# Issuing the moves of h ahead of the column loads, and placing its transposes one half-step later

## The chip, the cores and the metric

The kernel runs on one core of one Trainium2 chip. The metric is the device time of one execution in microseconds (us). Before the change the median of three runs is 1601.92 us (1600.87 to 1601.97).

## The reference, cut to what matters

There are B = 16 sequences x of 512 rows (S) by 512 columns (D), all in f32. Each passes through two parts:

```python
# part A: pooled attention of one sequence, and the layer norm behind it
attn_in = tanh(x @ W1 + b1)                      # 512 x 128
scores  = attn_in @ v                            # 512
p       = softmax(where(mask, scores, -1e30))    # prefix, postfix or cloze mask, by itok
pooled  = (p @ x) / count_of_the_mask            # 512 x 512
h       = layernorm(pooled) * gamma + beta
# part B: feed-forward, F = 2048, weights dequantized from integer codes
y   = silu(h @ w1 + fc1_bias)                    # 512 x 2048
z   = y @ w2 + fc2_bias                          # 512 x 512
out = x + pooled + 0.5 * z
```

## The kernel before, in words

Every matmul of f32 values is made from two parts in the type fp32r: a rounded copy ("hi") and the rest ("lo"). A product takes three matmuls, hi by hi, hi by lo and lo by hi. All dequantized weights stay in SBUF.

The program is written out by hand for each engine; semaphores join the engines. `ffn(b)` exists on TensorE, VectorE and ScalarE and does part B of sequence b, with the steps of part A of sequence a = b + 1 set between. On TensorE it has 28 half-steps h (0 to 27, `LAST`). An even h issues `fc1(b, h/2 + 2)`, 12 matmuls of 512 columns that make one 128-row piece k of the hidden layer in one of two PSUM banks `y_ps` (lines 1045 to 1047). An odd h issues `fc2(b, (h-1)/2)`, 12 matmuls that add piece k into the four banks `z_ps` (lines 1079 to 1081). Behind the half-steps come `fc2(b, 14)`, `fc2(b, 15)`, and `fc1(b+1, 0)` and `fc1(b+1, 1)` of the next sequence. The turn from one sequence to the next is called a transition here.

Between `fc1(b, k)` and `fc2(b, k)` stand two steps. ScalarE's `silu(b, k)` (line 561) waits for the matmuls of fc1 and writes `y_f`; it is placed at the even half-step h = 2(k - 2), so silu(b, 15) stands at h = 26. VectorE's `split_y(b, k)` (lines 849 and 851) makes `y_hi` and `y_lo` from it; it waits for silu and for `fc2(b, k-2)`, whose operands it overwrites. It is placed at h = 2(k - 1): split_y(b, 14) at h = 26, split_y(b, 15) at h = 28. Each engine runs its own list strictly in order. At every half-step the silu or split comes first and then the steps which the tables `ACT_STEADY` and `DVE_STEADY` name for that half-step.

The layer norm of the next sequence ends on VectorE with `normalise` (step "H", h = 20, line 800). The transposed h that fc1 needs is reached in one of two ways. For a = 0 and a = 1 TensorE transposes it (`by_pe`). For a = 2 to 15 it goes by these steps:

- `move_h(a)` on SyncE (line 364) waits for `h_ready` and issues 16 DMAs of 64 KB from `scratch` to `h_cols`; they move blocks of 32 by 32 to their transposed places.
- `turn_h(a, c)`, "TURNH" on VectorE (line 807): four transposes within the blocks, `h_cols` to `scratch`. The first waits until all 16 moves have landed (`h_moved`).
- `h_scaled_rows(a, c)`, "AFFINE" on ScalarE (line 551): four times gamma and beta, in place.
- `split_h(a, c)` on VectorE (lines 814 and 816): `hT_hi` and `hT_lo`. c = 0 and 1 stand in the table ("SPLITH", h = 27, so ahead of split_y(b, 15)), c = 2 and 3 behind the loop.

TURNH and AFFINE both stand at h = 25, so ahead of split_y(b, 14) on VectorE and ahead of silu(b, 15) on ScalarE.

SyncE issues the other DMAs too. `turn(b, p)` is its list for one sequence, run for b = 1 to 14: wait until the pooling matmuls of sequence b have read `xs_hi` and `xs_lo` (`xs_used`; `x_cols` lies in the same memory), issue the 16 pieces of 64 KB of `load_columns(b + 1)` (line 323), then `move_h(b)` where b is 2 or more, then four stores of sequence b - 1 (line 328) and four loads of x of sequence b + 1 (line 376). `move_h(15)` stands alone behind the list. The `x_cols` are read by VectorE's "TURN" (line 686) at h = 0 to 2 of `ffn(b)`, which is the half-step 0 of the sequence after the moves. `h_cols` lies in the memory of `part_hi`, `part_lo`, `coef` and `u_rows`.

Of the kernel before, what the change touches and what calls it, by code (L numbers as in the profile page):

```python
# [18 lines left out]
def build(nc, x, itok, cond_w, cond_b, cond_v, gamma, beta, fc1_q, fc1_s, fc1_b, fc2_q, fc2_s, fc2_b, out):  # L19
# [16 lines left out]
    with ExitStack() as ctx:  # L36
# [112 lines left out]
        def bank(name):  # L149
# [106 lines left out]
                     17: [("PZ", 2)], 18: [("PZ", 3)]}  # L256
        ACT_STEADY = {0: [("XT", 0)], 1: [("XT", 1)], 2: [("XT", 2)], 3: [("XT", 3)], 4: [("TANH", 0)], 5: [("SC", 0)],
                      9: [("EXPE", 0), ("EXP", 0)], 11: [("U", 0)], 15: [("PZ", 0)], 16: [("PZ", 1)], 17: [("PZ", 2)],
                      18: [("PZ", 3)], 25: [("AFFINE", 0), ("AFFINE", 1), ("AFFINE", 2), ("AFFINE", 3)]}
        DVE_STEADY = {0: [("TURN", 0), ("TURN", 1), ("XT", 0)], 1: [("TURN", 2), ("XT", 1)], 2: [("TURN", 3), ("XT", 2)],  # L260
                      3: [("XT", 3)], 4: [("PAR", 0)], 5: [("SCAN", 0)], 6: [("COLS", 0)], 7: [("ROWMAX", 0)],
# [3 lines left out]
                      25: [("TURNH", 0), ("TURNH", 1), ("TURNH", 2), ("TURNH", 3)], 27: [("SPLITH", 0), ("SPLITH", 1)]}  # L265

        def by_pe(a):
            return isinstance(a, int) and a <= 1
# [39 lines left out]
        @block.sync  # L308
        def _(sp):
            x_dram = x.rearrange("b (j p) d -> (b j) p d", p=P)  # L310
            out_dram = out.rearrange("b (j p) d -> (b j) p d", p=P)

            def load_x(a, p, blocks):
                for J in blocks:
                    sp.dma_start(xt[p][:, J, :], x_dram[bass.ds(a * NJ + J, 1), :, :].rearrange("a p d -> p (a d)")).then_inc(x_in[p][J], 16)

            x_split = x.rearrange("b (i q) d -> b q i d", q=Q)

            def load_columns(a):
                for s in range(ND):  # L320
                    for j in range(P // Q):
                        cols = slice(s * P + j * Q, s * P + (j + 1) * Q)
                        sp.dma_start(x_cols[s][j * Q:(j + 1) * Q, :].rearrange("q (i d) -> q i d", d=Q),  # L323
                                     x_split[bass.ds(a, 1), :, :, cols].rearrange("a q i d -> q (a i) d")).then_inc(cols_in[s], 16)

            def store(b, p, J):
                sp.wait_ge(final_done, b * NJ + (J + 1))
                sp.dma_start(out_dram[bass.ds(b * NJ + J, 1), :, :].rearrange("a p d -> p (a d)"), xt[p][:, J, :]).then_inc(stored[J], 16)

            NG = NF // ND  # L330

            def load_w1(g):
                cols = slice(g * NG * P, (g + 1) * NG * P)
                sp.dma_start(q1[:, :, cols], fc1_q[:, cols].rearrange("(c p) f -> p c f", p=P)).then_inc(w1_in[g], 16)
                sp.dma_start(s1[:, :, cols], fc1_s[:, cols].rearrange("(o k) f -> o k f", o=1).to_broadcast([P, ND, NG * P])).then_inc(w1_in[g], 16)

            def load_w2(g):
                rows = slice(g * NG, (g + 1) * NG)
                sp.dma_start(q2[:, rows, :], fc2_q[g * NG * P:(g + 1) * NG * P, :].rearrange("(k p) d -> p k d", p=P)).then_inc(w2_in[g], 16)
                sp.dma_start(s2[:, rows, :], fc2_s[rows, :].rearrange("(o k) d -> o k d", o=1).to_broadcast([P, NG, D])).then_inc(w2_in[g], 16)  # L340

            load_x(0, 0, range(2))
            sp.dma_start(wc_f.rearrange("p (c a) -> p c a", c=ND), cond_w.rearrange("(c p) a -> p c a", p=P)).then_inc(wc_in, 16)
            sp.dma_start(tok_i[:], itok.rearrange("(o d) -> o d", o=1).to_broadcast([P, B])).then_inc(tok_in, 16)
            load_x(0, 0, range(2, NJ))
            load_w1(0)
            load_w2(0)
            sp.dma_start(b2h[:], fc2_b.rearrange("(o d) -> o d", o=1).to_broadcast([P, D])).then_inc(bias_in, 16)
            load_w1(1)
            load_x(1, 1, range(NJ))  # L350
            load_w2(1)
            sp.wait_ge(xs_used, NJ)
            load_columns(1)
            for g in range(2, ND):
                load_w1(g)
                load_w2(g)

            def move_h(a):
                rows = scratch[:, 0:NJ * D].rearrange("p (n d) -> p n d", d=P)
                sp.wait_ge(h_ready, a * NJ + NJ)  # L360
                for i in range(P // Q):
                    for j in range(P // Q):
                        piece = slice(j * Q, (j + 1) * Q)
                        sp.dma_start(h_cols[piece, :, i * Q:(i + 1) * Q], rows[i * Q:(i + 1) * Q, :, piece]).then_inc(h_moved, 16)  # L364

            def turn(b, p):

                sp.wait_ge(xs_used, (b + 1) * NJ)
                load_columns(b + 1)
                if not by_pe(b):  # L370
                    move_h(b)
                for J in range(NJ):
                    store(b - 1, p, J)
                for J in range(NJ):
                    sp.wait_ge(stored[J], b * 16)
                    sp.dma_start(xt[p][:, J, :], x_dram[bass.ds((b + 1) * NJ + J, 1), :, :].rearrange("a p d -> p (a d)")).then_inc(x_in[p][J], 16)

            turn(1, 0)
            turn(2, 1)
            with sp.Fori(1, B // 2 - 1) as i:  # L380
                turn(i * 2 + 1, 0)
                turn(i * 2 + 2, 1)
            move_h(B - 1)
            for b in (B - 2, B - 1):
                for J in range(NJ):
                    store(b, b % 2, J)
            for J in range(NJ):
                sp.wait_ge(stored[J], 16 * B)
# [786 lines left out]
```

## Time and profile before

| what | value |
|---|---|
| median of three runs | 1601.92 us |
| the profiled execution's own time | 1604.28 us |
| its span, first to last instruction | 1602.5 us |
| TensorE busy in the span | 1578.7 us (99%) |
| VectorE busy | 954.0 us (60%) |
| ScalarE busy | 431.6 us (27%) |
| mean granted TensorE clock | 0.999 |

"Busy" counts a matmul from its start to its modelled end, 0.39 us; when matmuls follow one another without a gap, the next one starts after 0.2267 us, while the one before still counts as busy. An idle time of TensorE in a row therefore leaves out the first 0.16 us of each gap.

### The profile page before, as it was taken

Reading aid. Unit: us, or ns where it says so; the run is one execution under the profiler, and the core shown is the slowest. Engines: PE = TensorE matmul, PEld = TensorE weight load, DVE = VectorE, ACT = ScalarE, POOL = GpSimd, SP = SyncE. Lnnn points to the kernel's source line nnn. Section 1 sums busy time; section 2 is a strip of 40 time slices with the busy share of each in tenths; the row PEclk is TensorE's granted clock in tenths of the full one; section 3 lists DMA queues with packets and bytes.
Section 4 is the critical chain, followed back from the end, with each engine's and each line's share of the span. In section 5 each row is a group of like instructions: output and inputs, shape, how many; then the busy total and the mean of one; then the engine's idle time right before and its main releaser. Section 6 shows DMA issues by size and latency. Waiting matters only on the chain.

```text
span 1602.5 us, 20995 instructions
## 1 busy us (share of the span) xinstructions
PE 1578.7 (99%) x7259; PEld 1268.9 (79%) x7259; DVE 954.0 (60%) x1918; ACT 431.6 (27%) x662; POOL 177.8 (11%) x156
## 2 busy tenths in 40 slices
PE   8999999999999999999999999999999999999999
PEld 5778788787887778787787877877878777887887
DVE  7896556655665565646656466555655656456522
ACT  3552322222231222312322223222222323123211
POOL 4101011110101101011110111101111010110100
PEclk9999999999999999999999999999999999999999
DMA  8803031130312204031040311303112031220200
GB/s 282 231 1 79 1 53 53 25 81 1 53 54 37 69 1 87 20 50 57 4 104 1 53 53 18 90 1 53 53 32 75 1 66 41 45 62 0 53 1 27
DMA packets 271311, 82.75 MB, mean 52 GB/s; under 512 B 247498, under 2 KB 248036, under 8 KB 270692
## 3 DMA queue, kind: packets, MB, share of 16 engines
q1 hardware_dynamic: 271152, 81.31, 21.4%
q8 instruction: 67, 1.10, 0.3%
q14 instruction: 40, 0.33, 0.1%
q10 hardware_dynamic: 52, 0.01, 0.0%
HBM read 49.83 MB, written 16.78 MB: 42 GB/s over the span
## 4 chain that ended last, share of the span: by engine, by line
PE 71%; SPq 14%; DVE 9%; issue 4%; DMA 2%; ACT 1%; DVEq 0%; ACTq 0%
PE y_ps L1045 11%; PE y_ps L1046 11%; PE y_ps L1047 11%; PE z_ps L1079 10%; PE z_ps L1080 9%; PE z_ps L1081 9%; SPq L364 8%; SPq L323 6%; DMA h_cols<-scratch 2%; DVE scratch L807 2%; DVE y_lo L851 1%; PE a_ps L1009 1%; PE a_ps L1011 1%; PE a_ps L1010 1%; PE a_ps L961 1%
## 5 line engine op out<-in xcount | busy, mean ns | idle before, releaser
L1079 PE MATMUL z_ps<-w_hi,y_hi 128*128 128x512 f32 x1024 | 402.0, 393 | 7.3 <-DVE y_lo L851 6.7
L1045 PE MATMUL y_ps<-hT_hi,w_hi 128*128 128x512 f32 x1016 | 406.4, 400 | 1.1 <-DVE w_lo L835 0.5
L561 ACT ACTIVATE y_f<-y_ps,vec_cols 128x512 f32<-128x512 f32 x256 | 176.2, 688 | 853.0 <-PE y_ps L1047 842.0
L1080 PE MATMUL z_ps<-w_lo,y_hi 128*128 128x512 f32 x1024 | 399.0, 390 | 0.0
L1081 PE MATMUL z_ps<-w_hi,y_lo 128*128 128x512 f32 x1024 | 398.9, 390 | 0.0
L1047 PE MATMUL y_ps<-hT_hi,w_lo 128*128 128x512 f32 x1016 | 396.9, 391 | 0.0
L1046 PE MATMUL y_ps<-hT_lo,w_hi 128*128 128x512 f32 x1016 | 396.9, 391 | 0.0
L1045 PEld LDWEIGHTS y_ps<-hT_hi,w_hi 128*128 128x128 f32 x1016 | 191.2, 188 | 60.2 <-issue 21.0
L1079 PEld LDWEIGHTS z_ps<-w_hi,y_hi 128*128 128x128 f32 x1024 | 192.3, 188 | 56.7 <-DVE y_lo L851 16.6
L1046 PEld LDWEIGHTS y_ps<-hT_lo,w_hi 128*128 128x128 f32 x1016 | 191.3, 188 | 41.8 <-issue 3.4
L1081 PEld LDWEIGHTS z_ps<-w_hi,y_lo 128*128 128x128 f32 x1024 | 192.3, 188 | 40.2
L1080 PEld LDWEIGHTS z_ps<-w_lo,y_hi 128*128 128x128 f32 x1024 | 192.4, 188 | 39.1 <-issue 0.2
L1047 PEld LDWEIGHTS y_ps<-hT_hi,w_lo 128*128 128x128 f32 x1016 | 191.1, 188 | 40.6
L849 DVE CAST y_hi<-y_f 128x512 fp32r<-128x512 f32 x240 | 112.8, 470 | 182.9 <-PE z_ps L1081 143.9
L851 DVE TENSOR_TENSOR y_lo<-y_f,y_hi 128x512 fp32r<-128x512 f32 x256 | 178.5, 697 | 20.7 <-ACT y_hi L480 12.4
L414 POOL TENSOR_TENSOR x<-x,scratch 128x512 f32<-128x512 f32 x64 | 83.2, 1302 | 872.6 <-ACT scratch L539 872.6
L422 POOL TENSOR_TENSOR x<-x,b2h 128x512 f32<-128x512 f32 x64 | 83.2, 1334 | 451.1 <-DVE hT_lo L816 413.3
L780 DVE BATCH_NORM_STATS2 stats<-scratch 128x6 f32<-128x512 f32 x64 | 44.4, 693 | 112.5 <-ACT scratch L539 112.5
L807 DVE STREAM_TRANSPOSE scratch<-h_cols 128x512 f32<-128x512 f32 x56 | 34.9, 680 | 87.3 <-DMA h_cols<-scratch 87.3
L539 ACT ACTIVATE scratch<-a_ps,columns 128x512 f32<-128x512 f32 x64 | 44.1, 689 | 97.1 <-PE a_ps L1014 95.3
L719 DVE TENSOR_TENSOR_SCAN scratch<-scratch 128x512 f32<-128x512 f32 x15 | 18.4, 1226 | 84.3 <-ACT scratch L480 84.3
L551 ACT ACTIVATE scratch<-scratch,vec_cols 128x512 f32<-128x512 f32 x56 | 41.1, 805 | 67.1 <-DVE scratch L807 67.1
(208 smaller groups left out, 1187.7 us busy)
## 6 DMA issues: line engine op xcount, KB each, us to landing
x<-in_x_dram SPq DMA_DIRECT2D x64, 256.0 KB, 3.4
out_dram<-x SPq DMA_DIRECT2D x64, 256.0 KB, 2.2
x_cols<-in_x_dram SPq DMA_DIRECT2D x240, 64.0 KB, 2.2
h_cols<-scratch SPq DMA_DIRECT2D x224, 64.0 KB, 2.1
fc_codes<-in_L_ffn_fc_q_dram SPq DMA_DIRECT2D x8, 1024.0 KB, 14.9
fc_scaled<-in_L_ffn_fc_scales_dram SPq DMA_DIRECT2D x8, 1024.0 KB, 16.3
scratch<-in_L_cond_W_dram SPq DMA_DIRECT2D x1, 256.0 KB, 4.3
b2h<-in_L_ffn_fc_bias_dram SPq DMA_DIRECT2D x1, 256.0 KB, 15.7
```

Source lines behind the costliest of these rows:

```text
L323: sp.dma_start(x_cols[s][j * Q:(j + 1) * Q, :].rearrange("q (i d) -> q i d", d=Q), x_split[bass.ds(a, 1), :, :, cols].rearrange("a q i d - ...
L364: sp.dma_start(h_cols[piece, :, i * Q:(i + 1) * Q], rows[i * Q:(i + 1) * Q, :, piece]).then_inc(h_moved, 16)
L414: nc.gpsimd.tensor_tensor(xt[p][:, J, :], xt[p][:, J, :], pooled[J], ALU.add).then_inc(res_added, 1)
L561: nc.scalar.activation(y_f[k % 2][:], y_ps[k % 2][:], ACT.Silu, bias=b1[:, k:k + 1]).then_inc(silu_done, 1)
L849: v.tensor_copy(y_hi[k % 2][:], y_f[k % 2][:]).then_inc(yhi_done, 1)
L851: v.tensor_tensor(y_lo[k % 2][:], y_f[k % 2][:], f32(y_hi[k % 2][:]), ALU.subtract).then_inc(split_done, 1)
L1045: mm(o, w1_hi[:, c, cols], hT_hi[:, c, :], start=(c == 0), stop=False)
L1046: mm(o, w1_hi[:, c, cols], hT_lo[:, c, :], start=False, stop=False)
L1047: last = mm(o, w1_lo[:, c, cols], hT_hi[:, c, :], start=False, stop=(c == ND - 1))
L1079: mm(z_ps[r][:], y_hi[k % 2][:, rows], w2_hi[:, k, :], start=(k == 0), stop=False)
L1080: mm(z_ps[r][:], y_hi[k % 2][:, rows], w2_lo[:, k, :], start=False, stop=False)
L1081: last = mm(z_ps[r][:], y_lo[k % 2][:, rows], w2_hi[:, k, :], start=False, stop=(k == NF - 1))
```

## The change

Two edits. In the tables of the steady sequences, the four steps AFFINE of ScalarE and the four steps TURNH of VectorE go from half-step 25 to 26. Since the silu and the split of a half-step come first, AFFINE then stands behind silu(b, 15) and TURNH behind split_y(b, 14). In SyncE's `turn`, `move_h(b)` goes ahead of the wait for `xs_used` and of `load_columns(b + 1)`.

```diff
         ACT_STEADY = {...
-                      18: [("PZ", 3)], 25: [("AFFINE", 0), ("AFFINE", 1), ("AFFINE", 2), ("AFFINE", 3)]}
+                      18: [("PZ", 3)], 26: [("AFFINE", 0), ("AFFINE", 1), ("AFFINE", 2), ("AFFINE", 3)]}
         DVE_STEADY = {...
-                      25: [("TURNH", 0), ("TURNH", 1), ("TURNH", 2), ("TURNH", 3)], 27: [("SPLITH", 0), ("SPLITH", 1)]}
+                      26: [("TURNH", 0), ("TURNH", 1), ("TURNH", 2), ("TURNH", 3)], 27: [("SPLITH", 0), ("SPLITH", 1)]}
...
             def turn(b, p):
 
+                if not by_pe(b):
+                    move_h(b)
                 sp.wait_ge(xs_used, (b + 1) * NJ)
                 load_columns(b + 1)
-                if not by_pe(b):
-                    move_h(b)
                 for J in range(NJ):
                     store(b - 1, p, J)
```

## Rows read from the trace of the kernel before

**Rows 1.** The page, busy time, share and count of TensorE.
```profile
PE 1578.7 (99%) x7259; PEld 1268.9 (79%) x7259; DVE 954.0 (60%) x1918; ACT 431.6 (27%) x662; POOL 177.8 (11%) x156
```

**Rows 2.** TensorE's waits from 200 to 1560 us: us in total, times, longest.
```profile
PE z_ps L1079 <- DVE y_lo L851: 6.7, 14, 1.3
```

**Rows 3.** Timeline of TensorE at one transition: start us, us, [idle before <-releaser].
```profile
527.70 0.39 PE L1079 MATMUL z_ps<-w_hi,y_hi 128*128 128x512 f32 x1
...
530.19 0.39 PE L1081 MATMUL z_ps<-w_hi,y_lo 128*128 128x512 f32 x1
531.30 0.50 PE L1079 MATMUL z_ps<-w_hi,y_hi 128*128 128x512 f32 x1 [0.72 <-DVE y_lo L851]
531.64 0.40 PE L1080 MATMUL z_ps<-w_lo,y_hi 128*128 128x512 f32 x1
...
533.92 0.39 PE L1081 MATMUL z_ps<-w_hi,y_lo 128*128 128x512 f32 x1
534.49 0.50 PE L1079 MATMUL z_ps<-w_hi,y_hi 128*128 128x512 f32 x1 [0.18 <-DVE y_lo L851]
```

**Rows 4.** The same timeline one transition earlier, end of fc2(b, 14), start of fc2(b, 15).
```profile
435.82 0.39 PE L1081 MATMUL z_ps<-w_hi,y_lo 128*128 128x512 f32 x1
436.32 0.50 PE L1079 MATMUL z_ps<-w_hi,y_hi 128*128 128x512 f32 x1
```

**Rows 5.** Timeline of VectorE around the transition of rows 3.
```profile
511.66 1.91 DVE L800 TENSOR_SCALAR scratch<-scratch,mv,columns 128x512 f32<-128x512 f32 x4
...
519.80 0.43 DVE L849 CAST y_hi<-y_f 128x512 fp32r<-128x512 f32 x1 [4.29 <-PE z_ps L1081]
...
527.72 2.49 DVE L807 STREAM_TRANSPOSE scratch<-h_cols 128x512 f32<-128x512 f32 x4 [6.76 <-DMA h_cols<-scratch]
...
531.16 0.42 DVE L814 CAST hT_hi<-scratch 128x512 fp32r<-128x512 f32 x1
...
533.29 0.42 DVE L849 CAST y_hi<-y_f 128x512 fp32r<-128x512 f32 x1
533.75 0.69 DVE L851 TENSOR_TENSOR y_lo<-y_f,y_hi 128x512 fp32r<-128x512 f32 x1
...
544.78 0.70 DVE L686 STREAM_TRANSPOSE scratch<-x_cols 128x512 f32<-128x512 f32 x1
```

**Rows 6.** Timeline of ScalarE around the transition of rows 3.
```profile
522.46 0.69 ACT L561 ACTIVATE y_f<-y_ps,vec_cols 128x512 f32<-128x512 f32 x1 [4.75 <-PE y_ps L1047]
528.47 2.93 ACT L551 ACTIVATE scratch<-scratch,vec_cols 128x512 f32<-128x512 f32 x4 [5.32 <-DVE scratch L807]
531.31 0.67 ACT L561 ACTIVATE y_f<-y_ps,vec_cols 128x512 f32<-128x512 f32 x1
```

**Rows 7.** Timeline of SyncE's DMA issues, same transition: start us, us.
```profile
506.07 8.74 SPq L323 DMA_DIRECT2D x_cols<-in_x_dram  x16
514.96 11.27 SPq L364 DMA_DIRECT2D h_cols<-scratch  x16
538.51 2.16 SPq L328 DMA_DIRECT2D out_dram<-x  x4
```

**Rows 8.** The same, the longest issue of 16 moves among the 14.
```profile
905.48 11.80 SPq L364 DMA_DIRECT2D h_cols<-scratch  x16
```

**Rows 9.** Timelines at the last transition: SyncE's moves, VectorE's transposes, TensorE's fc2(b, 15).
```profile
1489.52 11.34 SPq L364 DMA_DIRECT2D h_cols<-scratch  x16
...
1502.34 2.49 DVE L807 STREAM_TRANSPOSE scratch<-h_cols 128x512 f32<-128x512 f32 x4 [5.29 <-DMA h_cols<-scratch]
...
1509.00 0.40 PE L1081 MATMUL z_ps<-w_hi,y_lo 128*128 128x512 f32 x1
1509.23 0.39 PE L1079 MATMUL z_ps<-w_hi,y_hi 128*128 128x512 f32 x1
```

**Rows 10.** The page, DMA issues: count, KB each, median us from issue to landing.
```profile
x_cols<-in_x_dram SPq DMA_DIRECT2D x240, 64.0 KB, 2.2
h_cols<-scratch SPq DMA_DIRECT2D x224, 64.0 KB, 2.1
```

## The prediction, made before the changed kernel was run

> **What bounds the kernel now.** I read the page first: TensorE is busy 1578.7 of 1602.5 us [rows 1]. So at most 24 us of visible idle can be had, and only what sits on TensorE counts. The waits came next, cut to the part behind the start-up (200 us on). The reader is to see that one wait is left there: fc2's first matmul for VectorE's y_lo, 14 times, 6.7 us in all [rows 2]. Third, the timeline of TensorE at a transition, where those waits lie. In a stream without gaps matmuls start 0.2267 us apart: 11 such steps lead from 527.70 to 530.19 [rows 3]. At the transition the first matmul of fc2(b, 14) starts 531.30 - 530.19 = 1.11 us after the one before it, which is 0.88 too much, the next one 0.34 after that, 0.11 too much, and fc2(b, 15) starts 534.49 - 533.92 = 0.57 after, 0.34 too much, with another 0.11 behind it. This transition loses 1.45 us, though its rows show only 0.72 + 0.18 as idle.
>
> Why: both wait for split_y. VectorE stands from 520.96 in front of TURNH, whose data land only at 527.72, and split_y(b, 14) is queued behind the four transposes [rows 5]. Its input (silu of 522.46 [rows 6]) and its buffer have been ready for long: the cast of split_y(b, 13) ran at 519.80 [rows 5], released by fc2, and one pair of half-steps is 24 x 0.2267 = 5.44 us, so split_y(b, 14) could run at 525.24. On ScalarE silu(b, 15) is queued behind the four AFFINE: it could run at 522.46 + 5.44 = 527.90 and runs at 531.31 [rows 6].
>
> **The whole loss.** There are 14 transitions by way of the moves (into sequences 2 to 15). Seven have two visible waits each: these are the 14 waits of 6.7 us in all. Each hides a further 0.39 - 0.23 = 0.16 us and costs 0.11 at the restart: 6.7 + 14 x 0.27 = 10.5 us. In six, only fc2(b, 15) is late and too little to show as idle: 436.32 - 435.82 = 0.50 us, 0.27 too much [rows 4], and 0.11 at the restart: 6 x 0.38 = 2.3 us. The last transition has no loss: 1509.23 - 1509.00 = 0.23 [rows 9]. Sum: 12.8 us.
>
> **What decides about a transition.** Call T the start of TURNH. In the old order fc2(b, 15) starts at T + 6.77 (534.49 - 527.72 [rows 3, 5]). In the last transition T = 1502.34 and the matmul is due at 1509.23, 6.89 later, so nothing waits [rows 9]. There SyncE had no column pieces ahead of its moves, and T is 1502.34 - 1489.52 = 12.82 us behind the first issue. This is the price of the moves in the changed order, already measured once.
>
> **First edit, the order on SyncE.** h is ready at 511.66 + 1.91 = 513.57 [rows 5]; the moves are first issued at 514.96, because the 16 pieces occupy the queue until 514.81 [rows 7]. Now they start at about 513.6, 1.3 us earlier. With 12.82 us from first issue to T, T = 526.4; with the longest issue seen (11.80 for 11.34 [rows 8, 9]) 526.9. The moves alone would by T + 6.77 put fc2(b, 15) at 533.2 to 533.7, against a due time of 527.70 + 5.44 = 533.14: most of the loss gone by this edit alone, a few tenths a transition left.
>
> Where a move's completion stands in relation to the pieces ahead of it, the trace shows 2.1 us from issue to landing as the median over all 224 moves [rows 10], and the last transition's moves, with nothing ahead of them, land no sooner: the last of 16 issues in 11.34 us starts about 0.7 before 1500.86, and T is 1502.34, 2.2 later [rows 9]. The Trainium skill (DMA: Bandwidth & Descriptors, Queues, rings and completion order) says that a semaphore increment lands only after every earlier write of the same DMA engine; by that the moves' count would be held up by column pieces ahead of them, and the edit would gain latency as well as queue time. The trace does not agree that any is to be had: by the rule T comes still earlier and rival 1 would have hardly a chance, by the rows it doesn't, and I take the rows.
>
> What is moved past what: the 16 column pieces, the wait for xs_used (fulfilled long before h is ready, since the pieces start at 506.07) and their landing now come behind the moves. Issue from 513.6 + 11.3 = 524.9 (525.4 with 11.80), 8.74 us long [rows 7], so until 533.6 to 534.2, landed 2.2 later [rows 10], 536. They are read by TURN at 544.78 [rows 5], in the faster kernel at 543.3: 7 us to spare. The stores behind them on SyncE's queue start at 538.51 [rows 7], about 537.1 then: 3 us to spare. Both cost nothing while this cover lasts. Bounds: 0, and 1 us a transition for each us by which the pieces land later than 543.3. I take 0; the pieces have to go wrong by 7 us.
>
> **Second edit, the order on VectorE and ScalarE.** split_y(b, 14) runs at 525.24 and takes 0.46 + 0.69 us [rows 5], done at 526.4. fc2(b, 14) is due at 527.70 + 2.72 = 530.42, so its wait is gone with 4 us to spare, whatever the moves do. TURNH then starts at the later of 526.4 and the landing, also 526.4 to 526.9. What is late next is fc2(b, 15), by one of two chains:
> - By VectorE: TURNH 2.49, two split_h 533.29 - 531.16 = 2.13, split_y(b, 15) 0.46 + 0.69, and 0.05 to the matmul [rows 3, 5], in all 5.82. For 533.14 T has to be at most 527.32. There are 0.4 to 0.9 us to spare.
> - By ScalarE: silu(b, 15) at 527.90, 0.69 long; AFFINE from 528.6, the first ends after 0.8 (2.93 for four [rows 6], one start each 0.7), at 529.4; then 2.13 + 1.15 + 0.05 as before: 532.7. 0.4 us to spare.
>
> So AFFINE behind silu(b, 15) costs nothing: it would start at 528.47 in the old order [rows 6], 528.6 in the new. The last two split_h run from 532.6 to 534.8, and fc1(b+1, 0) is due at 533.14 + 2.72 = 535.86, needing its fourth chunk 2 us after that. Without the first edit T would stay 527.72 and fc2(b, 15) would come at 533.5, 0.4 late: the second edit alone keeps a loss of about 0.4 + 0.11 in the seven bad transitions. Bounds of this edit: nothing lost, or, if ScalarE's chain takes 0.7 us more than summed, 0.3 + 0.11 in each of 14, 5.7 us.
>
> **Sum.** No instruction is added or taken away; 12.8 us of gaps go. The profiled execution, 1604.28 us with a span of 1602.5, would become 1591.5 and 1589.7. The runs have a median of 1601.92, 2.4 lower than the profiled one; the gaps are the same in kind, so the median becomes 1601.92 - 12.8 = 1589.1. In the gapless stream at 0.23 instead of 0.2267 per matmul around transitions there may be another 1 or 2 us either way.
>
> **Rivals.**
> 1. fc2(b, 15) stays late. For it: both chains have only 0.4 us of slack, built of ten small instructions. Against it: all their durations come from the same place of the trace. Price 0.41 x 14 = 5.7 us: 1594.8.
> 2. The loss is only handed on, and TensorE waits just as long somewhere behind the transition, or SyncE spends the 1.3 us in longer issues (the same 16 moves took 11.27, 11.80 and 11.34 us). Against it: the last transition, which has the new order on SyncE, has neither wait. Price: the gain, 12.8 us; 1601.9, or 1599 where a part is kept.
> 3. Slower: the column pieces come too late for TURN, VectorE stands in front of it at half-step 0 and the splits behind it on VectorE starve fc2. It begins to cost when the pieces land after 543.3, and outweighs the gain when they are late by more than 12.8 / 13 = 1.0 us in each of the 13 turns that have both moves and pieces, landing after 544.3 against 536 as summed. With 2 us of lateness: 1589.1 + 26 = 1615. For it: issue times on this queue scatter. Against it: by a few us at most in 16 issues.
>
> **How the numbers follow.** A measurement of this kernel tells about 0.2%, 3.2 us, from no change. The forecast, all gaps gone, 1586.5 to 1591.5: chance 0.63. Rival 1, about 1592 to 1597: 0.20. Rival 2: 0.11, of which 0.02 still faster. Rival 3: 0.06. Faster by over 0.2% is 0.63 + 0.20 + 0.02 = 0.85, within 0.2% 0.09, slower 0.06. Range: 1586.5 to 1595.5, which holds the forecast's case and most of rival 1.
>
> **What would show it.** In the trace after: no wait of fc2 for y_lo behind 200 us (14 before); the cast of split_y(b, 14) 5.44 us behind that of split_y(b, 13) and ahead of TURNH; moves issued within 0.1 us of the end of line 800, pieces behind them; T about 12.8 us behind the first move; matmul starts 0.23 apart through the transition; TURN without a wait for a DMA. The prediction is wrong if fc2(b, 15) still waits, if TURN waits for x_cols, or if the gaps are gone and the span is not 11 to 14 us shorter.

## The result and the profile after

The changed kernel takes 1589.71 us, the median of four runs (1589.08 to 1590.59), against 1601.95 us for four runs of the kernel before: 12.2 us less, ratio 0.9918 (95% interval 0.9905 to 0.9930). The forecast was 1589.1, the range 1586.5 to 1595.5. Run again in a later set it had a median of 1589.92 beside 1603.31, ratio 0.9915 (0.9901 to 0.9928).

The page after, busy times; 6.5 us less of busy TensorE time for the same 7259 matmuls, the part of the gaps which counts as busy [rows 1].
```profile
span 1587.8 us, 20995 instructions
PE 1572.2 (99%) x7259; PEld 1270.0 (80%) x7259; DVE 952.1 (60%) x1918; ACT 431.8 (27%) x662; POOL 178.1 (11%) x156
```

TensorE's waits between 200 and 1545 us: after, the view has no row, and fc2 waits for VectorE nowhere. Before, it has the row of 6.7 us in 14 times [rows 2] and a second one:
```profile
PE y_ps L1045 <- issue: 0.4, 2, 0.2
```
These two waits lie at the jumps of TensorE's loop (639.43 and 834.76), where the changed kernel's profile has gaps too small to show; they differ from profile to profile and have nothing to do with the edits.

The same transition as in rows 3, now about 3.6 us earlier on the clock. TensorE: end of fc2(b, 14), start of fc2(b, 15).
```profile
526.82 0.39 PE L1079 MATMUL z_ps<-w_hi,y_hi 128*128 128x512 f32 x1
...
529.32 0.39 PE L1081 MATMUL z_ps<-w_hi,y_lo 128*128 128x512 f32 x1
529.54 0.39 PE L1079 MATMUL z_ps<-w_hi,y_hi 128*128 128x512 f32 x1
529.77 0.39 PE L1080 MATMUL z_ps<-w_lo,y_hi 128*128 128x512 f32 x1
```
Where rows 3 have 0.57 and 0.34 us between starts, these have 0.22 and 0.23.

VectorE, to be read against rows 5:
```profile
508.06 1.91 DVE L800 TENSOR_SCALAR scratch<-scratch,mv,columns 128x512 f32<-128x512 f32 x4
...
516.21 0.43 DVE L849 CAST y_hi<-y_f 128x512 fp32r<-128x512 f32 x1 [4.29 <-PE z_ps L1081]
...
521.65 0.43 DVE L849 CAST y_hi<-y_f 128x512 fp32r<-128x512 f32 x1 [4.29 <-PE z_ps L1081]
522.11 0.69 DVE L851 TENSOR_TENSOR y_lo<-y_f,y_hi 128x512 fp32r<-128x512 f32 x1
522.72 2.48 DVE L807 STREAM_TRANSPOSE scratch<-h_cols 128x512 f32<-128x512 f32 x4
525.82 0.43 DVE L814 CAST hT_hi<-scratch 128x512 fp32r<-128x512 f32 x1 [0.61 <-ACT scratch L551]
...
527.95 0.42 DVE L849 CAST y_hi<-y_f 128x512 fp32r<-128x512 f32 x1
528.40 0.69 DVE L851 TENSOR_TENSOR y_lo<-y_f,y_hi 128x512 fp32r<-128x512 f32 x1
```
The cast of split_y(b, 14) comes 521.65 - 516.21 = 5.44 us behind the one before and ahead of TURNH. TURNH no longer waits for the moves. The wait has gone to the first split of h, 0.61 us for AFFINE, which costs nothing: split_y(b, 15) ends at 529.09, 0.05 is the way to the matmul, and fc2(b, 15) is due at 529.54. This is a slack of 0.4 us.

ScalarE and SyncE, to be read against rows 6 and 7:
```profile
524.30 0.69 ACT L561 ACTIVATE y_f<-y_ps,vec_cols 128x512 f32<-128x512 f32 x1 [4.75 <-PE y_ps L1047]
524.89 2.92 ACT L551 ACTIVATE scratch<-scratch,vec_cols 128x512 f32<-128x512 f32 x4
```
```profile
510.00 11.06 SPq L364 DMA_DIRECT2D h_cols<-scratch  x16
521.35 8.34 SPq L323 DMA_DIRECT2D x_cols<-in_x_dram  x16
533.42 2.16 SPq L328 DMA_DIRECT2D out_dram<-x  x4
```
The moves start 0.03 us behind the end of line 800 (508.06 + 1.91 = 509.97), and the pieces end 3.7 us before the stores begin.

How much of the time it is: 13 whole sequences, from the scores of sequence 2 to those of sequence 15 (first column), before and after. Columns: stretch, its length, then busy times.
```profile
171.19:1439.99 1268.80, 1261.04 (x5799) 1014.51 (x5798) 753.06 (x1547) 328.17 (x507) 132.63 (x104) 1.00 0.20 44
```
```profile
170.85:1425.33 1254.48, 1254.48 (x5800) 1015.49 (x5799) 751.18 (x1547) 328.31 (x507) 132.74 (x104) 1.00 0.20 44
```
14.3 us went in these 13 sequences. In the other runs of this study the same stretch tells more than the whole time, since the first sequence varies by 1.2 us from one profile to another (91.8 or 93.0 us from its scores to the next). The same kernel profiled twice differs by 0.7 us in it (1254.48, and 1255.15 for `again` below).

Counted from start to start, some 11 us of other gaps behind 200 us are left in the changed kernel. They stand at the same places as before, 0.8 us a sequence, the largest 0.41 us right behind the score matmuls; the change does not touch them.

### The profile page after: what moved, and what is told of

It reads as the page before. It is cut to its first block, busy times and chain, and to the rows that moved or that the text cites. A ratio compares the mean times of both kernels' runs of the same rounds, so it can differ in the third digit from the quotient of the medians.

```text
span 1587.8 us, 20995 instructions
## 1 busy us (share of the span) xinstructions
PE 1572.2 (99%) x7259; PEld 1270.0 (80%) x7259; DVE 952.1 (60%) x1918; ACT 431.8 (27%) x662; POOL 178.1 (11%) x156
## 4 chain that ended last, share of the span: by engine, by line
PE 93%; DVE 5%; ACT 1%; issue 1%; DMA 0%; SPq 0%; DVEq 0%; ACTq 0%
PE y_ps L1045 14%; PE z_ps L1079 14%; PE z_ps L1080 14%; PE z_ps L1081 14%; PE y_ps L1046 14%; PE y_ps L1047 14%; PE a_ps L1009 1%; PE a_ps L1014 1%; PE a_ps L1011 1%; PE a_ps L1010 1%; PE a_ps L960 1%; PE a_ps L962 1%; PE a_ps L961 1%; PE a_ps L977 1%; PE a_ps L966 1%
## 5 line engine op out<-in xcount | busy, mean ns | idle before, releaser
L849 DVE CAST y_hi<-y_f 128x512 fp32r<-128x512 f32 x240 | 109.6, 457 | 246.7 <-PE z_ps L1081 204.0
L860 DVE TENSOR_TENSOR x<-z_ps,x 128x512 f32<-128x512 f32 x64 | 40.0, 683 | 20.5 <-PE z_ps L1081 20.5
L691 DVE TENSOR_TENSOR part_lo<-scratch,part_hi 128x512 fp32r<-128x512 f32 x30 | 20.7, 690 | 48.7 <-ACT part_hi L480 48.7
## 6 DMA issues: line engine op xcount, KB each, us to landing
b2h<-in_L_ffn_fc_bias_dram SPq DMA_DIRECT2D x1, 256.0 KB, 15.6
```

What stands on the lines that cost most here:

```text
L849: v.tensor_copy(y_hi[k % 2][:], y_f[k % 2][:]).then_inc(yhi_done, 1)
```

## The experiments

Theory A: a transition costs what VectorE's split_y(b, 15) comes too late for fc2(b, 15), and that follows from T, the start of TURNH, by a chain whose length the order of steps sets: T + 6.77 in the old order, T + 5.8 in the new; the order on SyncE sets T. The rivals: one of the two edits carries the gain; the slack is nothing; the wait is handed on. Medians of five runs or more; the kernel before ran beside each, in three sets on three chips, and its medians differ by 0.6 us between them. "13 seq." is the stretch of above.

| kernel | median | before | ratio (95%) | 13 seq. |
|---|---|---|---|---|
| sp_only | 1592.10 | 1603.46 | 0.9930 (0.9917 to 0.9944) | 1255.90 |
| steps_only | 1593.71 | 1603.46 | 0.9939 (0.9925 to 0.9953) | 1259.30 |
| sp_turnh | 1589.98 | 1603.46 | 0.9915 (0.9902 to 0.9929) | 1255.34 |
| sp_affine | 1591.18 | 1603.46 | 0.9926 (0.9913 to 0.9940) | 1256.18 |
| again (the changed kernel) | 1589.92 | 1603.31 | 0.9915 (0.9901 to 0.9928) | 1255.15 |
| more_work | 1603.23 | 1603.31 | 0.9999 (0.9990 to 1.0008) | 1268.36 |
| cols_behind_stores | 1598.36 | 1603.31 | 0.9973 (0.9963 to 0.9983) | 1262.99 |
| cols_behind_loads | 1655.98 | 1603.31 | 1.0329 (1.0315 to 1.0343) | 1320.36 |
| split_behind | 1589.77 | 1603.89 | 0.9912 (0.9899 to 0.9926) | 1255.07 |
| split_behind_sp | 1590.26 | 1603.89 | 0.9916 (0.9902 to 0.9929) | 1254.29 |

### Each edit alone

sp_only, the changed kernel with the steps put back:
```diff
-26: [("AFFINE", 0), ...]      -26: [("TURNH", 0), ...]
+25: [("AFFINE", 0), ...]      +25: [("TURNH", 0), ...]
```


> Only the moves of h go ahead of the column pieces; TURNH and AFFINE stay at half-step 25. Theory A (everything hangs on T, the start of TURNH; each order only has its own latest T): the changed kernel's trace gives first issue of the moves 0.03 us behind line 800, 10.7 us of issue in one parity and 11.1 to 11.4 in the other, and 1.49 from the end of the issue to T. In the frame in which split_y(b,13) runs at 519.80 this is T = 525.8 and 526.1 to 526.5. The old order needs T + 6.77 for fc2(b,15), due 533.14, so T up to 526.37: no gap in most transitions, 0.1 to 0.2 us in a few. Time about 1590 to 1591, one or two visible gaps at most. Rival B (the reordering of the steps carries the gain): most of the 12 us are back, 1597 or more. My prediction before had put T at 526.4 to 526.9 with this edit, 0.1 to 0.5 us lost in each: 1593.

11.4 us under the kernel before, 2.2 over the changed one. Its waits of TensorE behind 200 us, us in total, times, longest:
```profile
PE z_ps L1079 <- DVE y_lo L851: 0.2, 1, 0.2
```
One visible gap in 14 transitions. TURNH and TensorE there, the transition with the longest issue of moves (11.71 us):
```profile
330.38 2.49 DVE L807 STREAM_TRANSPOSE scratch<-h_cols 128x512 f32<-128x512 f32 x4 [5.83 <-DMA h_cols<-scratch]
...
337.15 0.50 PE L1079 MATMUL z_ps<-w_hi,y_hi 128*128 128x512 f32 x1 [0.19 <-DVE y_lo L851]
```
337.15 - 330.38 = 6.77, the same chain as in rows 3 and 5 to the hundredth. Three other transitions have gaps of 0.08 to 0.25 us, too small to show as idle. Rival B falls: this edit alone brings most of the time.

The expectation of 1590 to 1591 was missed by 1.1 us. With the restarts the four gaps come to 1.2 us; sp_only took 2.1 us more than sp_turnh of the same set (1589.98), which has no gap. What the other 0.9 us are is not shown.

This run also shows T bare, since TURNH waits for the landing in every transition. The moves of one transition and the TURNH behind them:
```profile
414.17 10.71 SPq L364 DMA_DIRECT2D h_cols<-scratch  x16
```
```profile
426.37 0.71 DVE L807 STREAM_TRANSPOSE scratch<-h_cols 128x512 f32<-128x512 f32 x1 [4.83 <-DMA h_cols<-scratch]
```
Here T is 12.20 us behind the first issue. In six transitions, every second one, it is 12.18 to 12.20, in the other eight 12.58 to 13.21; behind the end of the issue it is 1.48 to 1.50 in all. A gap appears exactly where the first figure is 12.85 or more, in four transitions.

steps_only, the kernel before with the tables of the changed one:
```diff
-25: [("AFFINE", 0), ...]      -25: [("TURNH", 0), ...]
+26: [("AFFINE", 0), ...]      +26: [("TURNH", 0), ...]
```


> Only TURNH and AFFINE go to half-step 26; the moves stay behind the column pieces. Theory A: T is as in the kernel before, 527.4 to 528.3 in the frame of rows 3 in the seven bad transitions and 526.7 in the others. fc2(b,14) is never late. fc2(b,15) comes at T + 5.82 against 533.14: late by 0.08 to 0.98 us in seven transitions (sum 3.3 of lateness and 0.11 each at the restart), on time in the others: 4 us over the changed kernel, 1593.8. Rival B (the steps carry the gain): 1590. Rival C (the moves carry it): 1600.

9.8 us under the kernel before, 3.8 over the changed kernel (1593.71 against 1589.92): theory A's 4 us, and neither rival's 0 or 10. fc2(b, 14) waits nowhere; fc2(b, 15) waits visibly in four transitions and a little in three more. The longest:
```profile
525.51 2.49 DVE L807 STREAM_TRANSPOSE scratch<-h_cols 128x512 f32<-128x512 f32 x4 [1.95 <-DMA h_cols<-scratch]
...
531.22 0.50 PE L1079 MATMUL z_ps<-w_hi,y_hi 128*128 128x512 f32 x1 [0.75 <-DVE y_lo L851]
```
The chain is 531.22 - 525.51 = 5.71 us; the prediction had summed 5.82. The two edits do not add: alone they bring 11.4 and 9.8, together 13.4 (1603.31 - 1589.92). Each makes the same wait shorter, from its own end, and either nearly suffices.

### Which of the two steps

sp_turnh leaves AFFINE at 25, sp_affine leaves TURNH at 25:
```diff
-26: [("AFFINE", 0), ...]      # sp_turnh, otherwise as changed
+25: [("AFFINE", 0), ...]
```
```diff
-26: [("TURNH", 0), ...]       # sp_affine, otherwise as changed
+25: [("TURNH", 0), ...]
```


> The moves first, TURNH at 26, AFFINE left at 25, ahead of silu(b,15). Theory A: AFFINE runs as TURNH comes, from about 527.0 to 530.0, silu(b,15) at 530 to 530.7, before VectorE wants it at 531: no gap, 1589.7, the same as the changed kernel. Here fc2(b,15) hangs on VectorE's chain alone, 532.2, and not on silu and AFFINE, 532.7: the move of AFFINE was of no use. Rival: a silu late by 2.8 us holds the split and costs 0.4 or more in each of 14: 1595.

> The moves first, AFFINE at 26 behind silu(b,15), TURNH left at 25, ahead of split_y(b,14). Theory A: TURNH starts at T = 525.8 to 526.5, split_y(b,14) follows and is ready at T + 3.6 = 529.4 to 530.1, before 530.42; the splits of h wait for T + 3.44 and for AFFINE (529.4); fc2(b,15) at T + 6.77 as in sp_only: 1590 to 1591. Rival: AFFINE behind silu(b,15) makes the splits of h later than in the old order and fc2(b,15) with them, 0.3 us in each: 1594.

sp_turnh is the changed kernel in time (1589.98, 1589.92), with no gap at any transition. Moving AFFINE behind silu(b, 15) brought no time; moving TURNH did all of the steps' part. This is shown with the moves first; neither step was moved alone in the old order of SyncE. VectorE in sp_turnh, to be read against that of the changed kernel:
```profile
521.26 0.43 DVE L849 CAST y_hi<-y_f 128x512 fp32r<-128x512 f32 x1 [4.29 <-PE z_ps L1081]
521.72 0.69 DVE L851 TENSOR_TENSOR y_lo<-y_f,y_hi 128x512 fp32r<-128x512 f32 x1
522.33 2.48 DVE L807 STREAM_TRANSPOSE scratch<-h_cols 128x512 f32<-128x512 f32 x4
524.74 0.38 DVE L814 CAST hT_hi<-scratch 128x512 fp32r<-128x512 f32 x1
...
526.83 0.42 DVE L849 CAST y_hi<-y_f 128x512 fp32r<-128x512 f32 x1
```
From split_y(b, 14) to split_y(b, 15) are 526.83 - 521.26 = 5.57 us, in the changed kernel 527.95 - 521.65 = 6.30. The first split no longer waits 0.61 us for AFFINE: the second half of the steps' edit took 0.7 us of slack, free as long as 0.4 are left. sp_affine has gaps like sp_only (0.34 us at two transitions, less at some others) and lies between the two; it and sp_only differ by 0.9 us in the median and by 0.3 us the other way in the 13 sequences, which is nothing that can be told apart.

### The slack, by added work

```diff
                 v.transpose(by_block(xt_rows[c]), chunk).then_inc(h_turned, 1)
+                if c == ND - 1:
+                    v.tensor_reduce(spare[:], by_block(b2h[:]), AX_X, ALU.max)
...
                 dve.wait_ge(hT_hi_done, a * ND + (c + 1))
+                if c < 2 and not by_pe(a):
+                    v.tensor_reduce(spare[:], by_block(b2h[:]), AX_X, ALU.max)
```


> The changed kernel with three reductions of 128x512 into a spare tensor added on VectorE at each of the 14 transitions: one behind TURNH, one inside each of the two splits of h that run ahead of split_y(b,15); 0.68 us each, 2.0 to 2.1 together. Nothing else waits for them. Theory A: VectorE's own chain ends at 526.35 + 5.82 = 532.2, the chain by ScalarE at 532.7, fc2(b,15) is due at 533.14: of 2.05 us added 0.97 are free, 1.08 are lost and 0.11 at the restart, 1.2 x 14 = 17 us over the changed kernel. Rival B (TensorE's time in these transitions is not set by VectorE at all): the same time. Rival C (no slack: each us added is a us lost): 30 us.

13.3 us over the changed kernel, not 17: the theory's kind, a size off. VectorE's chain in one transition:
```profile
428.24 2.48 DVE L808 STREAM_TRANSPOSE scratch<-h_cols 128x512 f32<-128x512 f32 x4
430.64 0.64 DVE L810 TENSOR_REDUCE spare<-b2h 128x4 f32<-128x512 f32 x1
431.33 0.43 DVE L817 CAST hT_hi<-scratch 128x512 fp32r<-128x512 f32 x1
431.79 0.69 DVE L820 TENSOR_REDUCE spare<-b2h 128x4 f32<-128x512 f32 x1
432.40 0.68 DVE L821 TENSOR_TENSOR hT_lo<-scratch,hT_hi 128x512 fp32r<-128x512 f32 x1
...
434.65 0.42 DVE L854 CAST y_hi<-y_f 128x512 fp32r<-128x512 f32 x1
435.11 0.69 DVE L856 TENSOR_TENSOR y_lo<-y_f,y_hi 128x512 fp32r<-128x512 f32 x1
```
With nothing to wait for, the next instruction starts 0.61 us after the start of one of 0.69 (431.79 to 432.40), so the three reductions add 1.9 us and not 2.05, to a chain of 5.71 and not 5.82. From T = 526.35 in the frame of rows 3 it ends at 526.35 + (435.80 - 428.24) + 0.05 = 533.96: 0.82 late, 0.11 at the restart, 13.0 us in 14. Counted from start to start, the 14 transitions of the trace lose 14.0 us. Of 1.9 us added, 1.1 are free: VectorE's own slack. Rivals B (0) and C (about 27) fall.

### The pieces still later

The 16 pieces and their wait behind the stores, or behind the loads too:
```diff
                 if not by_pe(b):
                     move_h(b)
-                sp.wait_ge(xs_used, (b + 1) * NJ)
-                load_columns(b + 1)
                 for J in range(NJ):
                     store(b - 1, p, J)
+                sp.wait_ge(xs_used, (b + 1) * NJ)     # cols_behind_stores; in cols_behind_loads
+                load_columns(b + 1)                   # these two stand behind the loads of x
```


> The 16 column pieces are issued behind the four stores of the sequence before instead of ahead of them, so from about 535.6 in the time of the changed kernel's trace (stores 533.42 to 535.58) instead of 521.35. Pieces for the first transpose land at 539.5, for the second at 541.5, the third 543.6, the fourth 546. TURN is due at 539.70, 540.3, 542.5 and 544.7, and the first projection at 543.14. Theory A: the first projection's operand is ready at 542.9, so 14 us of delay of the pieces cost nothing, 0 to 0.3 us a transition: the time of the changed kernel, up to 3 us more. Rival 3 of my prediction in a strict form (any lateness of the pieces is paid): 13 x 1.2 = 16 us more.

8.4 us over the changed kernel: half the strict price, and well over theory A's 0 to 3. In one parity of the loop the expectation held and no time went. In the other it failed; TURN, and the first projection on TensorE:
```profile
444.31 0.71 DVE L686 STREAM_TRANSPOSE scratch<-x_cols 128x512 f32<-128x512 f32 x1 [1.80 <-DMA x_cols<-in_x_dram]
445.78 0.71 DVE L686 STREAM_TRANSPOSE scratch<-x_cols 128x512 f32<-128x512 f32 x1 [0.76 <-DMA x_cols<-in_x_dram]
...
447.12 0.50 PE L960 MATMUL a_ps<-part_hi,wc_hi 128*128 128x512 f32 x1 [0.64 <-DVE part_lo L691]
```
```profile
438.44 9.74 SPq L323 DMA_DIRECT2D x_cols<-in_x_dram  x16
```
The first four pieces landed 444.31 - 438.44 = 5.9 us after the first issue, where I had counted 4.0. In the other parity the first TURN finds its pieces 3.8 to 4.0 us after the first issue. The 16 issues take 9.7 to 10.4 us in the late parity within the loop, 8.4 in the other.

> The 16 column pieces are issued behind the four stores and the four loads of x too, from about 538.3 in one parity and 540 to 541 in the other (the loads take 2.5 or 4.1 to 5.3 us there). First pieces land at 542.1 or 544, the second four 2.2 later, the first projection's operand is ready 1.3 behind that, 545.6 or 547.5, against 543.14 due. Theory A: 2.5 to 4.5 us lost in each of 13 or 14 sequences, 35 to 60 us more than the changed kernel: slower than the kernel before, as rival 3 said, with TensorE's first projection waiting for VectorE and VectorE for the DMA. Rival: the lateness is taken up by the half-steps behind (VectorE is 60% busy): under 10 us more.

66 us over the changed kernel, 53 over the kernel before: rival 3 of the prediction, made to happen, and somewhat worse than expected (35 to 60). TensorE's waits:
```profile
PE a_ps L960 <- DVE part_lo L691: 43.1, 13, 4.6
```
3.3 us each. Three stretches around one of them; columns: stretch, length, TensorE busy and count, and, third from the end, the granted clock:
```profile
440.00:457.95 17.95, 17.57 (x78) 14.21 (x77) 10.15 (x18) 4.24 (x7) 5.04 (x4) 1.00 0.44 130
462.35:465.38 3.03, 3.03 (x7) 2.41 (x8) 2.06 (x4) 0.04 (x1) 0.00 (x0) 0.53 0.61 95
465.38:480.00 14.62, 14.62 (x64) 11.75 (x63) 5.00 (x13) 3.70 (x6) 0.00 (x0) 1.00 0.00 0
```
Behind a wait of 4.0 us the granted clock has a mean of 0.53 for 3.0 us, about the level of 1.2 GHz, in which TensorE did 7 matmuls instead of 13. Counted start to start, the 13 waits cost 45.1 us; behind nine of them matmuls follow 0.43 us apart, which costs 15.6 us more (18.9 with the restarts and the matmuls between the two levels). This second part was in no expectation, and it is what the result has above the middle of the range.

### A shorter chain instead

The first two splits of h behind split_y(b, 15), on top of steps_only (split_behind) and of the changed kernel (split_behind_sp):
```diff
-27: [("SPLITH", 0), ("SPLITH", 1)]}
+28: [("SPLITH", 0), ("SPLITH", 1)]}
```


> The order of SyncE's queue as in the kernel before (pieces first, moves behind), TURNH and AFFINE at 26, and the first two splits of h moved from half-step 27 to 28, behind split_y(b,15). Theory A (a transition is lost or not by VectorE's chain from T to the end of split_y(b,15)): the chain loses its 2.13 us for the two splits and becomes 2.49 + 1.15 + 0.05 = 3.7, so T may be as late as 529.4, against 528.3 as the latest seen; silu(b,15) is ready at 528.6. fc1(b+1,0) is due at 535.86 and gets its first chunk by 533 and its last by 536.2, due 537.9. No gap, 1590, 13.4 us under the kernel before, with SyncE's order as it was. Rival B (the moves have to come first for the last microseconds): 1593 to 1594, as with the steps alone.

1589.77, 14.1 us under the kernel before: with SyncE's queue left as it was, the whole gain is there. TURNH and split_y(b, 15) of one transition:
```profile
524.03 2.49 DVE L807 STREAM_TRANSPOSE scratch<-h_cols 128x512 f32<-128x512 f32 x4 [1.47 <-DMA h_cols<-scratch]
526.84 0.43 DVE L849 CAST y_hi<-y_f 128x512 fp32r<-128x512 f32 x1 [0.32 <-PE z_ps L1081]
```
The moves are late here (VectorE waits 1.47 us for them), and it doesn't matter: split_y(b, 15) goes as soon as fc2(b, 13) frees its buffer.

> The changed kernel with the first two splits of h at 28, behind split_y(b,15). Theory A: no gap is left that this could remove; 2.1 us more of slack for fc2(b,15), and the time of the changed kernel, 13.4 us under the kernel before, within 0.1%. Rival: later hT makes fc1(b+1,0) wait, 0.3 to 1 us in each of 14: 1594 to 1600.

1590.26, the changed kernel within 0.1%, no wait of TensorE. There is nothing left at the transitions: three kernels end at the same time by different ways, none beats the changed one measurably.

## Why the prediction was right

1. The bound: "only what sits on TensorE counts", and of that only the 14 waits of rows 2. Right in substance. That "one wait is left there" was not exact: the view has a second row, 0.4 us at two jumps of the loop, which is gone in this profile after and back in that of `again` (0.3 us, once).
2. The whole loss, 12.8 us, from 6.7 us that the rows show as idle, by counting start to start (0.16 hidden under each modelled end, 0.11 at each restart, and six transitions whose gap isn't shown at all). Measured: 12.2 and 13.4 us in the medians, 14.3 in the profiles. Taking the 6.7 at its word would have missed half. The rest of the 14.3 is not in the transitions' large gaps: the jumps of TensorE's loop, 1.4 us before and 0.7 after by the same counting, come out differently in each profile, and a remainder of 0.8 us is spread over steps of 0.22 to 0.24 us and is too small to place. These were the "1 or 2 us either way". The spans of the two profiles differ by 14.7 us (1602.5 and 1587.8), which lies just outside the prediction's own sign, "11 to 14 us shorter": the profile before was 2.4 us above its median, as the prediction had said, and the one after was not.
3. T. Predicted 526.4 to 526.9 in the frame of rows 3, from the last transition's 12.82. Measured bare in sp_only it is 12.2 us behind the first issue in six transitions and 12.6 to 13.2 in eight, which is 525.8, and 526.2 to 526.8. The last transition was taken as the price, and it is on the slow side (its issue took 11.34 us before, 11.86 after; in every second transition 10.7). So this term was 0.6 us too long in six transitions, and it is why sp_only shows gaps in four transitions and not a few tenths in each (1592.1 measured, some 1593 by the prediction's T). The trace before already had the two sizes: T is 12.2 us behind the first issue in the six transitions with small gaps and 12.3 to 13.3 in the others.
4. The two chains to fc2(b, 15): by ScalarE 0.4 us to spare, predicted and read; by VectorE 5.82 predicted and 5.71 measured, slack 1.1 by added work where 0.4 to 0.9 was predicted.
5. "AFFINE behind silu(b, 15) costs nothing": right, and sp_turnh adds that it gains nothing.
6. "... the second edit alone keeps a loss of about 0.4 + 0.11 in the seven bad transitions", 3.6 us: 3.8 measured.
7. The pieces: TURN never waits in the changed kernel, as forecast. The pieces can be 14 us later for 8.4 us in all. By the prediction's bound, 1 us for each us behind 543.3, it would have been some 90 us (536 + 14 is 7 us behind, 13 times): the bound took all 16 pieces as due at once, while the first TURN needs four of them. What is late beyond is paid about once, with the clock's part on top.
8. The landing of the moves. T is 1.47 to 1.50 us behind the end of the moves' issue in all 14 transitions of the kernel before, 13 of them with the pieces ahead of the moves (527.72 - 526.23 = 1.49 [rows 5, 7]), and 1.48 to 1.50 in the 14 of sp_only with none ahead. The first edit gained queue time and no latency, as the prediction took it from the rows. The Trainium skill (DMA: Bandwidth & Descriptors, Queues, rings and completion order) says that a semaphore increment lands only after every earlier write of the same DMA engine. No run here shows this rule at work, or tells against it. The prediction read a gain in latency out of it, but by its own rows the rule would have given none: the pieces' issue is over at 514.81 [rows 7], their landing 2.2 us later at the median [rows 10], about 517 as an estimate, and the last move is issued some 8 us after that.

## What to carry to other kernels

Where a pipelined engine is 99% busy, count its gaps from start to start: here 6.7 us of shown idle were 12.8. Then ask of each wait how long the chain behind its releaser is and when the last input of that chain comes; an instruction that waits on a late DMA doesn't belong ahead of work that is already due. Two edits that shorten the same wait do not add up, and the cheapest may be enough (here split_behind, which changes only the order of steps in the tables). Before a duration is carried over from one occurrence, all its occurrences in the trace should be read: the 14 issues of moves came in two sizes.

## What the runs showed that was not expected

- Behind nine of the 13 waits of TensorE in cols_behind_loads the granted clock fell to the lower level, for 5 to 13 matmuls (1.0 to 2.6 us lost each). Those nine were of 2.8 to 4.8 us, start to start less one matmul; the four without it of 2.2 to 3.2, so here the length of the wait alone does not tell. Behind the gaps of the kernel before, of at most 1.5 us, nothing of the kind is seen: the matmuls follow after 0.34 and then 0.23 us, as in rows 3.
- In the changed kernel's loop, 16 equal issues of pieces take 8.3 to 8.4 us in one parity of a two-sequence loop body and 9.1 to 9.6 in the other; the 16 of moves take 10.7 us where the pieces take long and 11.1 to 11.5 where the pieces are quick. What sets it stays open; no run varied it.
